# Local attention of a six-part decoder stack: where the normaliser's square stands, and how two kinds of sums are formed

## What is computed

```
x: (4, 1024, 512);  16 heads of 32;  window of 128 earlier tokens
g = x @ Wg.T + bg;  v = x @ Wv.T + bv          # per head
corr[i,j] = (g_i . g_j) / (|g_i||g_j| + 1e-8) * m[i,j];  corr = (corr + 1) / 2
gene_means_i = mean_j corr[i,j];  denom = gene_means + 0.5
sum_inv = sum_i 1/denom_i
gene_fitness_i = 1 / (denom_i * sum_inv)
attn = softmax_j( corr * gene_fitness_i  where m, else -1e10 )
out = (attn @ v) @ Wo.T + bo
x = layernorm(x + out)
```

## Time and profile before

| | us |
|---|---|
| median of three runs | 2727.08 |
| profiled execution | 2725.91 |
| its span | 2724.2 |
| PE busy in the span | 2599.2 (95%) |
| DVE busy | 1906.9 (70%) |
| ACT busy | 810.2 (30%) |
| POOL busy | 867.6 (32%) |

### The profile page before, as it was taken

One profiled execution on the slowest core, in us unless ns is written; L12 is line 12 of the kernel. 1 busy time (PEld: TensorE's weight loads), 2 busy tenths in 40 slices (PEclk: granted clock), 3 DMA queues, 4 the chain that ended last, 5 costly groups with the idle time before them and its releaser, 6 DMA issues. The chain is left out here.

```text
span 2724.2 us, 37190 instructions
## 1 busy us (share of the span) xinstructions
PE 2599.2 (95%) x13149; PEld 1587.4 (58%) x13149; DVE 1906.9 (70%) x3326; ACT 810.2 (30%) x1197; POOL 867.6 (32%) x900
## 2 busy tenths in 40 slices
PE   8999998999998889999988879999999999999998
PEld 4444545555555444555544447777777777777775
DVE  4788404666667336666678758888888888888886
ACT  1111322333322245666678511111111111111110
POOL 2232104454454346767678611001111111111000
PEclk9999999999999999999999979999999999999999
DMA  5444130000000133333335501111111111111111
GB/s 173 147 172 146 57 120 1 1 1 1 1 1 1 55 95 94 101 99 96 100 105 144 170 29 41 45 45 45 45 44 40 43 44 44 40 40 45 40 39 37
DMA packets 218916, 175.95 MB, mean 65 GB/s; under 512 B 37839, under 2 KB 184655, under 8 KB 217710
## 3 DMA queue, kind: packets, MB, share of 16 engines
q1 hardware_dynamic: 188054, 148.59, 18.4%
q10 hardware_dynamic: 30680, 24.98, 3.3%
HBM read 90.51 MB, written 52.43 MB: 52 GB/s over the span
## 5 line engine op out<-in xcount | busy, mean ns | idle before, releaser
L2092 PE MATMUL bank<-tiles,tl_XQT 128*128 128x512 f32 (+1 forms) x768 | 327.6, 570 | 0.0
L2097 PE MATMUL bank<-tiles,tl_XQT 128*128 128x512 f32 (+1 forms) x768 | 318.0, 557 | 0.0
L2109 PE MATMUL bank<-tiles,tl_HT 128*128 128x512 f32 x682 | 306.3, 605 | 1.6 <-DMA tl_HT<-tl_tmp 1.6
L2097 PEld LDWEIGHTS bank<-tiles,tl_XQT 128*128 128x128 f32 x768 | 236.9, 308 | 65.4
L2092 PEld LDWEIGHTS bank<-tiles,tl_XQT 128*128 128x128 f32 x768 | 232.4, 310 | 62.0 <-issue 8.5
L2109 PEld LDWEIGHTS bank<-tiles,tl_HT 128*128 128x128 f32 x682 | 218.2, 325 | 73.6 <-issue 8.7
L1401 POOL TENSOR_SCALAR_AFFINE_SELECT tiles<-tiles 128x512 f32<-128x512 f32 x256 | 181.7, 712 | 183.4 <-ACT tiles L1636 168.2
L2044 POOL TENSOR_TENSOR tl_rs<-tl_ve,mhalf 128x1 f32<-128x1 f32 x29 | 15.9, 550 | 549.7 <-DVE tl_ve L2244 549.7
L2168 ACT ACTIVATE tl_HQ<-bank 128x512 f32<-128x512 f32 (+1 forms) x96 | 53.9, 562 | 410.6 <-PE bank L2092 381.5
L1743 DVE SCALAR_TENSOR_TENSOR tiles<-tiles,bank 128x1024 f32<-128x1024 f32 (+1 forms) x128 | 141.7, 1148 | 21.8 <-PE bank L1505 21.7
L1406 POOL TENSOR_SCALAR_AFFINE_SELECT tiles<-tiles 128x512 f32<-128x512 f32 x224 | 153.8, 686 | 0.0
(11 more groups left out here) (303 smaller groups left out, 4962.5 us busy)
## 6 DMA issues: line engine op xcount, KB each, us to landing
tl_HT<-tl_tmp SPq DMA_DIRECT2D x248, 44.0 KB, 1.9
tl_HT<-tl_tmp ACTq DMA_DIRECT2D x248, 44.0 KB, 2.0
fp_weights<-space_quant ACTq DMA_DIRECT2D x33, 256.0 KB, 2.0
X<-in_x SPq DMA_DIRECT2D x8, 1024.0 KB, 10.6
v<-tiles SPq DMA_DIRECT2D x32, 256.0 KB, 2.4
unit_g<-tiles SPq DMA_DIRECT2D x32, 256.0 KB, 2.4
unit_gT<-tiles SPq DMA_DIRECT2D x32, 256.0 KB, 2.8
la_GN<-unit_g SPq DMA_DIRECT2D x128, 64.0 KB, 1.9
```

The lines of the kernel that those rows point to most:

```text
L2092: mm = e.matmul(bank[(2 * q) % 3][:, 0:w], chunk(XQT[n % 2], c), WgT[q][:, :, c, :], start=(c == 0), stop=(c == C - 1))
L2097: mm = e.matmul(bank[(2 * q + 1) % 3][:, 0:w], chunk(XQT[n % 2], c), WuT[q][:, :, c, :], start=(c == 0), stop=(c == C - 1))
L2109: mm = e.matmul(bank[DOWN][:, :], chunk(HT, q), WdT[:, q, :], start=(q == 0), stop=(q == IC - 1))
```

## The change

Three edits, all in `local_attention`.

1. ScalarE: `normaliser(x // 2)` goes ahead of `tanh(p + 1)` in rounds where m > NT (NT = 32), which is p >= 92, and where the pair is not the first of a chunk. Elsewhere it stays last.
2. The sums over tokens of the unit vectors (`gsum`) are no longer formed by `tile_sums` from GT for half a chunk at a time. `token_sums(m)` forms them once for each projected tile from GQ, for its four groups of heads, at the end of VectorE's R0 and R4 (tile m - 2 of that round). `pair_sums(b)` makes the sums of neighbouring tiles once for each batch. gsum and gpair hold all 128 columns. `unit_transposed`, which overwrites GQ, waits for `token_sums` of the tile two before. `z` now holds the wait for the load of GT.
3. `inverse`: the second product takes its sum over tokens along (`accum_out`), and the separate sum L1777 is gone, with its wait.

```
@@ scalar
+                    ahead = there(x) and not first(x) and m > NT
+                    if ahead:
+                        normaliser(x // 2)
                     if there(p):
                         tanh(p + 1)
...
-                    if there(x) and not first(x):
+                    if there(x) and not first(x) and not ahead:
                         normaliser(x // 2)
@@ unit_transposed
+                    e.wait_ge(s_gs.sem, s_gs.at(m - 1))
@@ vector
-                def tile_sums(n, h):
-                    tiles = slice(HG * h, HG * h + HG)
-                    e.wait_ge(d_gt[n % 2][h].sem, d_gt[n % 2][h].at(16 * (n // 2 + 1)))
-                    e.tensor_reduce(gsum[:, tiles], GT[n % 2][:, h * D:(h + 1) * D]..., AX.X, ALU.add)
-                    ...
+                def token_sums(m):
+                    b, g = m // G, m % G
+                    e.wait_ge(s_gc.sem, s_gc.at(m + 1))
+                    e.tensor_reduce(gsum[...][:, :, g], GQ[m % 2].rearrange("p (c q) -> p c q", c=C), AX.X, ALU.add)
+                def pair_sums(b):
+                    e.wait_ge(s_gs.sem, s_gs.at(G * (b + 1)))
+                    e.tensor_copy(at(gpair)[:, :, 0:1], at(gsum)[:, :, 0:1])
+                    e.tensor_tensor(at(gpair)[:, :, 1:G], at(gsum)[:, :, 0:G - 1], at(gsum)[:, :, 1:G], ALU.add)
@@ z: gpair[:, t:t + 1] -> gpair[:, n * G + t:n * G + t + 1]; waits for pair_sums of the batch, and for GT
@@ inverse
                     e.scalar_tensor_tensor(out=ZZ[:, x], in0=GS[n % 2][:, x], scalar=1.0, in1=ZZ[:, x],
-                                           op0=ALU.add, op1=ALU.mult).then_inc(s_inv.sem, 1)
-                    e.wait_ge(s_inv.sem, s_inv.at(at + 1))
-                    e.tensor_reduce(S2[:, h:h + 1], ZZ[:, x], AX.X, ALU.add).then_inc(s_f0.sem, 1)
+                                           op0=ALU.add, op1=ALU.mult, accum_out=S2[:, h:h + 1]).then_inc(s_f0.sem, 1)
@@ vector's round
                         z(here(HG), 0)
-                        tile_sums(here(HG), 1)
...
-                    if here(0) is not None:
-                        tile_sums(here(0), 0)
+                    if here(0) is not None and here(0) % C == 0:
+                        pair_sums(here(0) // C)
...
                         if tile(m):
                             biased(m)
+                        if tile(m - 2):
+                            token_sums(m - 2)
```

More of the change, by code:

```diff
@@ L1206, in local_attention @@
         BO, half = sb("BO", [P, P]), sb("half", [P, 1])
-        gsum, gpair = sb("gsum", [P, G]), sb("gpair", [P, G])
+        gsum, gpair = sb("gsum", [P, NC * G]), sb("gpair", [P, NC * G])
         S2, S, S4, rS = sb("S2", [P, 2]), sb("S", [P, 1]), sb("S4", [P, 1]), sb("rS", [P, 1])
@@ L1226, in local_attention @@
         s_s0, s_sq, s_ao, s_a0 = (sem(n) for n in ("first_sums", "normaliser", "out", "first_out"))
-        s_gs, s_gp, s_z, s_S, s_den, s_u4, s_i0, s_inv = (sem(n) for n in (
-            "tile_sums", "pair_sums", "z", "S_mm", "denominator", "fourth_power", "inverse_step", "inverse"))
+        s_gs, s_gp, s_z, s_S, s_den, s_u4, s_i0 = (sem(n) for n in (
+            "token_sums", "pair_sums", "z", "S_mm", "denominator", "fourth_power", "inverse_step"))
         s_f0, s_f1, s_f2, s_f3, s_gse = (sem(n) for n in ("half_sum", "sum_inverse", "sum_inverse4", "fitness_share", "scaled"))
@@ L1743, in scores, with z @@
                     e.scalar_tensor_tensor(out=y, in0=y, scalar=1.0, in1=d, op0=ALU.add, op1=ALU.mult).then_inc(s_u.sem, 1)
-                def tile_sums(n, h):
-                    tiles = slice(HG * h, HG * h + HG)
-                    e.wait_ge(d_gt[n % 2][h].sem, d_gt[n % 2][h].at(16 * (n // 2 + 1)))
[L1748 to L1758, removed]
+                def token_sums(m):
+                    b, g = m // G, m % G
+                    e.wait_ge(s_gc.sem, s_gc.at(m + 1))
+                    e.tensor_reduce(gsum[:, b * C * G:(b + 1) * C * G].rearrange("p (c t) -> p c t", c=C)[:, :, g],
+                                    GQ[m % 2].rearrange("p (c q) -> p c q", c=C), AX.X, ALU.add).then_inc(s_gs.sem, 1)
+                def pair_sums(b):
+                    at = lambda v: v[:, b * C * G:(b + 1) * C * G].rearrange("p (c t) -> p c t", c=C)
+                    e.wait_ge(s_gs.sem, s_gs.at(G * (b + 1)))
+                    e.tensor_copy(at(gpair)[:, :, 0:1], at(gsum)[:, :, 0:1]).then_inc(s_gp.sem, 1)
+                    e.tensor_tensor(at(gpair)[:, :, 1:G], at(gsum)[:, :, 0:G - 1], at(gsum)[:, :, 1:G], ALU.add).then_inc(s_gp.sem, 1)
+                def z(n, h):
+                    e.wait_ge(s_gp.sem, s_gp.at(2 * (n // C) + 2))
+                    e.wait_ge(d_gt[n % 2][h].sem, d_gt[n % 2][h].at(16 * (n // 2 + 1)))
                     e.wait_ge(s_gat.sem, s_gat.at(G * n + HG * h + HG))
@@ L1762, in z @@
                         i = e.scalar_tensor_tensor(out=ZZ[:, t * P:(t + 1) * P], in0=bank[WB][:, (t % HG) * P:(t % HG + 1) * P],
-                                                   scalar=gpair[:, t:t + 1], in1=GT[n % 2][:, t * P:(t + 1) * P],
+                                                   scalar=gpair[:, n * G + t:n * G + t + 1], in1=GT[n % 2][:, t * P:(t + 1) * P],
                                                    op0=ALU.add, op1=ALU.mult)
```

## The result

The changed kernel takes 2733.3 us (median of 19 runs, 2729.2 to 2734.7); beside it the kernel before took 2726.8 (19 runs, 2722.7 to 2728.5). The ratio is 1.0023, with a 95% interval of 1.0016 to 1.0030: slower by about 6.3 us (the medians differ by 6.5). The forecast was 2727.9, within 2722.5 to 2731.5. The profiled execution took 2733.46 us, its span 2731.6, against 2724.2 before: +7.4.

The account below looks back on a forecast made before the run. PE bounds the stage with projections; without them, a loop through in-order queues does. Square +1.8 and +1.44, inverse -2.48, others nothing: +0.76 on the median 2727.08 gives 2727.9 us, range 2722.5 to 2731.5 for 8 in 10.

Parts of the forecast that it names:

- Unchanged stage with projections, token sums hidden there: Chunks with projections: PE sets the pace, 37.92 us unchanged to 0.2; token sums fit with 0.2 us to spare.
- Rival (d): Beside projections, between `biased` and `out` in R0 and R4: token sums not hidden, +16 us if fully exposed, 2743; chance 0.06.
- The shift of the tanh, 0.36 in R0: R0 to R4 without projections: the square ahead delays tanh, `sums` and `denominator` by 0.36 us, four times, +1.44.
- R2's place at nothing: Square ahead of R2's tanh costs nothing, being just level with R4's `arguments(p)` behind `dots`; otherwise 0.1 to 0.3 us, four times.
- If the slack is gone in R4 and R0, the square waits and the tanh with it, by at most 0.1 to 0.3 us each: Square's new wait on PE's `attend(x + 1)`: R0 has 0.3 us of slack; without it, a delay up to that bound.
- both shift together: `attend(x + 1)` and ACT's readiness for the square move together with the scores, as `projections` holds that matmul until they are done.
- Saved: 0.62 us, four times: R2's inverse, R0 to R4: dropping L1777's 0.72 us for an accumulator taken as 0.1 gives -2.5 us; bounds -2.9 and -0.1.
- `tile_sums` "Nothing": R4 and R0 without projections: removing `tile_sums`, about 1.0 us of DVE in each, changes nothing in the time.
- (a): Rival: the tanh's shift is hidden by a later releaser of `sums`; only the inverse counts, -2.5 us, 2724.6; chance 0.12.
- (b): Rival: DVE sets the period without projections, -21 us, 2706; partial form -6, 2721; chance 0.09, half of it partial.
- (c): Rival: the inverse's accumulator costs a whole pass, 0.69 us instead of 0.1, +3.1 in all, 2730.2; chance 0.15.
- (e): Rival: the square's edit does nothing because no pair is ahead; m > 32 holds in 18 rounds; no chance given.

Follow-up runs that it names:

- e1: The changed kernel with the square back behind the second tanh in every round: 2726.8 us, ratio 0.9999 to the kernel before.
- e9: The changed kernel with R2's `dots` made twice, same values, in the rounds without projections: 2730.3 us, ratio 1.0012 to the kernel before.
- e2: The kernel before with only the square moved ahead of the second tanh where nothing is projected: 2733.2 us, ratio 1.0023 to the kernel before.
- e5: The changed kernel with the square ahead of the second tanh in R2 alone: 2727.1 us, ratio 0.9997 to the kernel before.
- e6: The changed kernel with the square ahead in R0 and R2 but not in R4: 2731.1 us, ratio 1.0009 to the kernel before.
- e12: The changed kernel with PE's second gather moved behind `attend(x)` in rounds without projections: 2732.0 us, ratio 1.0017 to the kernel before.
- e3: The kernel before with only the accumulator in place of the separate sum over the inverse: 2726.7 us, ratio 1.0001 to the kernel before.
- e4: The kernel before with the token sums edit alone: 2729.3 us, ratio 1.0009 to the kernel before.
- e15: e4 with POOL's masks on exp(s + 1) in R6 without projections replaced by a small memset: 2726.7 us, ratio 0.9999 to the kernel before.
- e10: e1 with PE's second gather moved behind `attend(x)` in rounds without projections: 2728.8 us, ratio 1.0007 to the kernel before.

## Why the prediction was wrong

The stretch without projections was forecast at +0.76 and came out at +6.17. The missing 5.41 us divide as follows, by the sums of the table. The accumulator and the token sums without the square's move (e1) gave -0.27 where -2.48 was forecast: 2.21. The square's move without a clock fall (e1 to e9) cost 3.93 where 3.24 was forecast: 0.69. The clock (e9 to the kernel after) cost 2.51, and the prediction had no term for it. e9 holds the repeated `dots` too, so the last two are as good as that repetition is free.

Its terms, beside the four R0 to R4 and five R4 to R0 of the kernel after:

- *Unchanged stage with projections, token sums hidden there*: right, 381.44 and 381.48. Rival (d) is out.
- *The shift of the tanh, 0.36 in R0*: right in size. 0.37 in e2 and in the decomposition, 0.36 between e5 and e6, and L1648's idle time grew to 1.28 (0.92 and 0.36; the 1.39 of the prediction adds the square's 0.47 instead).
- *R2's place at nothing*: right in sum (e5), though not by standing still: R0 to R4 is 0.5 shorter, R4 to R0 0.5 longer, because R4's `arguments(p)` now waits for R2's tanh.
- **"If the slack is gone in R4 and R0, the square waits and the tanh with it, by at most 0.1 to 0.3 us each"**: this step failed. In R0 there was no wait. In R4 it is 0.86 us, nearly three times the bound, and R4's place costs 0.57 us (e6 to the kernel after) where 0.36 was forecast, 2.54 us in the five. I read the slack from R0's row (1482.28 + 0.40 against 1482.97) and carried it to R4, where it was 0.19 (1470.83 against 1471.02); "both shift together" holds for the scores, but `attend(x + 1)` has a gather ahead of it whose releaser is POOL's mask of a tanh that the same change makes later one round earlier. e12 shows 0.6 us of it. That the exponentials start 0.31 later is R2's place (e5).
- **The clock was taken as full**, the largest error. A longer wait of PE was priced at its own length. In two chunks the wait of 0.95 (0.58 before) behind one of 0.77 to 0.85 was followed by half clock, and R0 to R4 took 1.15 and 1.29 us more than in e9: 2.5 us in all. It was no rival of mine.
- **"Saved: 0.62 us, four times"**: the instruction is cheaper than I took it (0.72 saved, a read of 0.08), but the term does not reach the end. e3 gives -0.6 and then +0.6. I followed the loop through ACT; a second one through POOL's masks and PE's second gather lay nearly level with it, so with the inverse earlier R4 waits for masks instead, which makes `denominator` 0.29 later, and the other 0.30 are the product beside a mask. e3's row, PE's second gather of R4:

```profile
1470.35 0.42 PE L1481 MATMUL bank<-tiles,la_GN 128*32 128x128 f32 x8 [0.41 <-POOL tiles L1406]
```

- **`tile_sums` "Nothing"** in R4 and R0: nothing in the queue, but 0.29 us per R4 to R0 by the product beside a mask (e4, e15), 1.4 us in five. A cost from an operation that was removed.

The sums: R4 to R0 went up by 6.34 where +1.8 was forecast; R0 to R4 by -0.17 where -1.04 was forecast, which is -2.6 without the clock (e9's 45.63 against 48.24) and +2.4 by the clock. Together +6.17 where +0.76 was forecast. Of the rivals, (a) is out, since the tanh's shift is there in e2; (b) is out, since DVE got emptier and the loop longer; (c) was wrong, since both products kept their 0.69 us; (e) is out, since the square's row at 1501.36 stands ahead of the tanh's. The Trainium skill ("VectorE: DVE Perf Modes", section "Two Vector instructions with no wait between them") is right that the accumulator is an instruction of its own. By line, 32 times:

```profile
L1780 DVE DVE_READ_ACCUMULATOR la_ZZ<-la_GS,la_ZZ 128x1 f32 x32 | 2.6, 81 | 0.0
```

Its price here is those 81 ns, and it starts 0.62 after the product. The halving that the Trainium skill states for two non-bf16 SBUF sources ("Vector Engine (DVE) Microarchitecture Reference", section 7) did not show, with an accumulator either: L1780 took 0.69 at 1518.44.

What stays open: why products and masks meet differently in every other chunk, so that 0.6 goes from one half to the other (13.58 and 12.98, 11.85 and 11.26), in e9 too, where no clock falls; why of four chunks with the same waits only one or two had the fall; and why the load of the values came late with the later gather.

## What to carry to other kernels

When three in-order queues are each 80 to 90% busy and the period repeats to 0.01 us, several loops are usually level: before you credit an edit, follow *every* operand of the next wait one round back, also through the engine that looks idle, and price a moved wait at the place where it lands, not at the one beside it where the row is handy. A longer wait of TensorE can cost the clock as well: here two waits of 0.8 and 0.95 us were followed by half clock in 6 of 16 places. Look for `PE` rows that doubled, and test it by filling the wait with repeated work. And test each part alone and on top of the others: here three parts forecast at +3.2, -2.5 and 0 us were worth +6.4, 0 and +1.4 alone.

## What the runs showed that I had not expected

- An operation of VectorE with two float32 operands in SBUF and a mask of GpSimd hold each other up: 128x128 from 0.29 to 0.47, 0.62 or 0.77 us; 128x512 (`scaled`) from 0.75 to 1.22; the mask from 0.64 to 1.10. The products L1776 and L1780, also with two SBUF operands, stayed at 0.69 where no mask ran (1517.77 to 1519.33). In the rows the one that starts later is the one that gets longer, by somewhat less than the other had still to run: below, the product by 0.21 us where the mask had 0.35 left, and the mask by 0.46 where the product had 0.60 left. That is why a shift of a few tenths of a us changes the product's time. First a product that starts in a mask, then a mask that starts in a product, both in the kernel before:

```profile
1462.15 0.63 POOL L1406 TENSOR_SCALAR_AFFINE_SELECT tiles<-tiles 128x512 f32<-128x512 f32 x1
1462.43 0.90 DVE L1770 SCALAR_TENSOR_TENSOR la_ZZ<-la_UU,la_ZZ 128x512 f32<-128x512 f32 x1
...
1476.04 0.69 DVE L1774 SCALAR_TENSOR_TENSOR la_ZZ<-la_GS,la_ZZ 128x512 f32<-128x512 f32 x1
1476.13 1.10 POOL L1401 TENSOR_SCALAR_AFFINE_SELECT tiles<-tiles 128x512 f32<-128x512 f32 x1 [1.57 <-ACT tiles L1636]
```

- The granted clock fell to 0.50, the 1.2 GHz level, for some 3 us (from 1439 to 1446 in e10), in the middle of a stage with PE 85% busy (107.17 of 126.02 us); repeated work ahead of the place went with a clock of 1.00 in all four chunks and a shorter time.
- The accumulator's read takes 81 ns, and the product with it still takes 0.69 us: from its start to the next instruction is 0.73 us, as before (1518.44 to 1519.17, 1487.19 to 1487.92).
